# Units of 256 places in place of 512 in the edge list of a graph attention layer

## What is computed

```python
x = x + conv2d(bfp_quantize(layernorm_channels(x)), bfp_quantize(w), bias)   # 16 x 64 x 56 x 56
t = tokens(x)                                   # 50,176 rows of 64
h = ln(t) @ W_gat                               # 16 numbers per node: 4 heads x 4 experts
e = leaky_relu(a_src[src] + a_dst[dst])         # 262,144 edges, 4 heads each
alpha = exp(e - e_max[dst]) / denom[dst]
agg = segment_sum(h[src] * alpha, dst)          # per node
w = softmax of the top 2 of 4 experts of mean_heads(layernorm(agg))
out = t + sum over 4 experts of w[e] * (gelu(t @ W1[e] + b1[e]) @ W2[e] + b2[e])
```

## Time and profile before

| | |
|---|---|
| median of 3 runs | 4735.66 us (4731.93 to 4740.96) |
| the profiled execution's own time | 4737.77 us |
| its span | 4736.0 us |
| mean granted TensorE clock | 0.820 |
| PE busy | 82% of the span |
| POOL busy | 60% |
| DVE busy | 56% |
| ACT busy | 20% |

### The profile page before, as it was taken

How to read it: one execution, slowest core, us unless ns; L and a number is a source line. 1 busy time by engine, 2 the same in 40 slices (tenths; PEclk the granted TensorE clock), 3 DMA queues, 4 the chain that set the end, 5 groups by cost and what they waited for, 6 DMA issues and landing times. The chain is left out here.

```text
span 4736.0 us, 62817 instructions
## 1 busy us (share of the span) xinstructions
PE 3866.3 (82%) x21121; PEld 2690.0 (57%) x21121; DVE 2657.0 (56%) x3261; ACT 942.1 (20%) x2069; POOL 2844.5 (60%) x2881
## 2 busy tenths in 40 slices
PE   4785333799948999999999999999999999661499
PEld 1453223577736666666666666666666667561122
DVE  7779999667644444444444444444444444447666
ACT  0110000000012333332333333333333333110000
POOL 2001888766626777777777777777777777771000
PEclk8897555788867888988888988889888888776699
DMA  1232111788862111111111111111111111682498
GB/s 48 69 96 74 49 47 35 85 107 102 102 107 49 34 35 34 36 35 35 35 35 35 35 35 35 35 33 37 32 38 33 35 35 34 10 10 3 137 289 247
DMA packets 323403, 284.04 MB, mean 60 GB/s; under 512 B 201074, under 2 KB 279154, under 8 KB 322804
## 3 DMA queue, kind: packets, MB, share of 16 engines
q1 hardware_dynamic: 213732, 200.98, 19.9%
q0 software_dynamic: 91008, 30.58, 11.5%
q10 hardware_dynamic: 18576, 51.39, 2.8%
HBM read 160.41 MB, written 122.31 MB: 60 GB/s over the span
## 5 line engine op out<-in xcount | busy, mean ns | idle before, releaser
L1074 POOL DMA_INDIRECT gath<-tab_d,src_no x2288 | 2158.9, 944 | 775.8 <-issue 696.9
L446 POOL DMA_INDIRECT edge_d<-run_slots,slots x544 | 657.2, 1208 | 662.8 <-ACT run_slots L636 502.2
L1204 PEld LDWEIGHTS C<-spread,lo_hot 128*128 128x128 f32 x4576 | 848.1, 244 | 331.3 <-DVE spread L1359 173.7
L1204 PE MATMUL C<-spread,lo_hot 128*128 128x160 f32 x4576 | 920.2, 370 | 139.4 <-DVE spread L1359 139.1
L1193 PEld LDWEIGHTS C<-dst_rows,lo_hot_t 128*128 128x128 f32 x4576 | 586.7, 208 | 91.1 <-issue 78.3
L1371 DVE TENSOR_TENSOR acc<-acc,C 128x160 f32 x572 | 183.5, 321 | 796.3 <-PE C L1204 746.8
L1193 PE MATMUL C<-dst_rows,lo_hot_t 128*128 128x32 f32 x4576 | 603.9, 289 | 11.2 <-ACT lo_hot_t L1092 11.2
L1214 PE MATMUL A<-T,w1s 64*128 64x392 f32 x1024 | 533.8, 605 | 0.0
L1097 ACT ACTIVATE hid<-A,b1s 128x392 f32<-128x392 f32 x512 | 300.6, 587 | 1078.9 <-PE A L1214 1078.9
L557 PE MATMUL C<-wide_rec,hot_lo 128*128 128x136 f16 x2048 | 266.8, 305 | 296.9 <-DVE wide_rec L814 296.9
L1225 PE MATMUL A<-hid,w2s 128*64 128x392 f32 x1024 | 456.3, 528 | 0.0
(11 more groups left out here) (263 smaller groups left out, 3195.6 us busy)
## 6 DMA issues: line engine op xcount, KB each, us to landing
mlp_d<-mlp ACTq DMA_DIRECT2D x128, 392.0 KB
mlp<-mlp_d SPq DMA_DIRECT2D x64, 784.0 KB, 4.7
gath<-tab_d,src_no POOLq DMA_INDIRECT x2288
pixels<-in_x SPq DMA_DIRECT2D x32, 392.0 KB, 8.1
src<-in_x SPq DMA_DIRECT2D x32, 392.0 KB, 9.2
T<-t_d SPq DMA_DIRECT2D x128, 98.0 KB
X<-x_d SPq DMA_DIRECT2D x64, 196.0 KB, 5.4
out<-X SPq DMA_DIRECT2D x128, 98.0 KB, 2.6
```

The lines of the kernel that those rows point to most:

```text
L446: pool.indirect_dma_start(edge_d, bass.IndirectOffsetOnAxis(ap=slots[:, k, c:c + 1], axis=0), run_slots[:, k, c * RUN:(c + 1) * RUN, :].re ...
L1074: pool.indirect_dma_start(gath[:, g % BUFS, j, :], None, tab_d, bass.IndirectOffsetOnAxis(ap=src_no[:, t:t + 1], axis=0)).then_inc(gathere ...
L1204: mm = pe.matmul(C[:, bank, at:at + HI * VALS], lo_hot[:, k, u * U + j, :], spread[:, u * U + j].rearrange("p h v -> p (h v)"), start=(j = ...
```

## The change

A unit is 2 tiles of 128, that is 256 places, and takes 64 runs of 4. Lane l below 64 holds places 0 and 1 of run l, lane 64 + l holds places 2 and 3 of it. A group is 8 units, still 16 tiles. Filling blocks up to whole units takes fewer places, and NG is 137, TILES 2,192. The list in DRAM has 64 rows, and it is loaded twice, once into each half of the lanes, each time with all 4 places of a run (`raw`, which lies in the space of `lo_hot`); each field is then read from it in two copies, one for each half. PSUM holds four units at a time (two banks of two), so the 8 units of a group go in 4 pairs through the two banks by turns, and PE waits before each pair until DVE has added the pair before the last (`pair_added`). In PE's `body` the first half's transposes stand ahead of step 2, and the second half of the scatters behind it.

```diff
-U = 4
-UNIT_RUN_BITS = 7
-UG = 4
+U = 2
+UNIT_RUN_BITS = 6
+RUN_ROWS = U * P // RUN
+PARTS_U = P // RUN_ROWS
+UG = 8
+PAIRS = UG // 2
...
-PLACES = TILES // RUN
-ALL_PLACES = PLACES + SG * RUN_COLS
+PLACES = NG * UG
+ALL_PLACES = PLACES + SG * RUN_COLS * P // RUN_ROWS
...
-        edge_d = dram("edge_d", [P * ALL_PLACES, RUN * FIELDS], F16)
+        edge_d = dram("edge_d", [RUN_ROWS * ALL_PLACES, RUN * FIELDS], F16)
...
-                n = TILES * FIELDS // 8
+                n = PLACES * RUN * FIELDS // 8
                 for k in range(8):
-                    pool.dma_start(edge_d.rearrange("(p n) e -> p (n e)", p=P)[:, k * n:(k + 1) * n], zeros_h[:, 0:n].bitcast(F16)).then_inc(s["pads_written"], 16)
+                    pool.dma_start(edge_d.rearrange("(p n) e -> p (n e)", p=RUN_ROWS)[:, k * n:(k + 1) * n], zeros_h[0:RUN_ROWS, 0:n].bitcast(F16)).then_inc(s["pads_written"], 16)
...
-            srt = tb("srt", [P, TILES, FIELDS], F16)
...
-                return 1 + u // 2, u % 2 * HI * VALS
+                return 1 + u // 2 % 2, u % 2 * HI * VALS
...
-            TRIPS = -(-NG // UNROLL)
-            LAST = NG - (TRIPS - 1) * UNROLL
+            TRIPS = (NG - 3) // UNROLL
+            LAST = NG - TRIPS * UNROLL
...
-                sp.dma_start(srt[:].rearrange("p c k -> p (c k)"), edge_d.rearrange("(p n) e -> p (n e)", p=P)[:, 0:TILES * FIELDS]).then_inc(s["sorted_loaded"], 16)
+                for h in range(PARTS_U):
+                    sp.dma_start(raw[h * RUN_ROWS:(h + 1) * RUN_ROWS], edge_d.rearrange("(p n) e -> p (n e)", p=RUN_ROWS)[:, 0:PLACES * RUN * FIELDS]).then_inc(s["sorted_loaded"], 16)
...
-                def scatter(g, k, units):
-
-                    if units[0] == 0:
+                def scatter(g, k, pairs):
+
+                    if pairs[0] == 0:
                         pe.wait_ge(s["spread_ready"], g + 1)
-                    for u in units:
-                        bank, at = bank_of(u)
-                        for j in range(U):
...
-                        if u % 2:
-                            mm.then_inc(s["scattered"], 1)
+                    for w in pairs:
+                        if w >= 2 or not (isinstance(g, int) and g == 0):
+                            pe.wait_ge(s["pair_added"], g * PAIRS + w - 1)
+                        for u in range(2 * w, 2 * w + 2):
+                            bank, at = bank_of(u)
+                            for j in range(U):
...
+                        mm.then_inc(s["scattered"], 1)
...
                     mlp_step(0)
-                    scatter(g, k, range(0, 2))
+                    scatter(g, k, range(0, PAIRS // 2))
                     mlp_step(1)
-                    scatter(g, k, range(2, UG))
-                    mlp_step(2)
                     if turns:
                         turn(g + 2, k2, 0)
+                    mlp_step(2)
+                    scatter(g, k, range(PAIRS // 2, PAIRS))
                     mlp_step(3)
...
-                L(dve.tensor_copy(mixed_i, srt[:].bitcast(U16)[:, :, 0]))
+                def field(v, dt):
+
+                    for h in range(PARTS_U):
+                        a = slice(h * RUN_ROWS, (h + 1) * RUN_ROWS)
+                        yield (mixed_i[a].rearrange("p (n t) -> p n t", t=U),
+                               raw[a].bitcast(dt).rearrange("p (n t v) -> p n t v", t=RUN, v=FIELDS)[:, :, h * U:(h + 1) * U, v])
+                for to, code in field(0, U16):
+                    L(dve.tensor_copy(to, code))
...
-                L(dve.tensor_copy(mixed_i, srt[:, :, 1]))
+                for to, place in field(1, F16):
+                    L(dve.tensor_copy(to, place))
...
                         if u % 2 == 0:
-                            dve.wait_ge(s["scattered"], g * 2 + bank)
+                            dve.wait_ge(s["scattered"], g * PAIRS + u // 2 + 1)
                         here = acc[:, bass.ds(qs[u], HI), :]
                         L(dve.tensor_tensor(here, here, C[:, bank, at:at + HI * VALS].rearrange("p (h v) -> p h v", h=HI), ALU.add))
+                        if u % 2:
+                            dve.sem_inc(s["pair_added"], 1)
```

More of the change, by code:

```diff
@@ L83 @@
 ID_W = -(-NG * UG // P)
-PLACES = TILES // RUN
-ALL_PLACES = PLACES + SG * RUN_COLS
-assert 1 << RUN_BITS == RUN and 1 << UNIT_RUN_BITS == U * P // RUN == P
+PLACES = NG * UG
+ALL_PLACES = PLACES + SG * RUN_COLS * P // RUN_ROWS
+assert 1 << RUN_BITS == RUN and 1 << UNIT_RUN_BITS == RUN_ROWS and PARTS_U * U == RUN
 BLKS = NB + 1
@@ L737, in _ @@
                 L(dve.tensor_reduce(start_b[:], runs, AX.X, ALU.add))
-                L(dve.tensor_scalar(units_i[:], start_b[:], float(P - 1), None, ALU.add))
+                L(dve.tensor_scalar(units_i[:], start_b[:], float(RUN_ROWS - 1), None, ALU.add))
                 L(dve.tensor_scalar(units_i[:], units_i[:], UNIT_RUN_BITS, None, ALU.arith_shift_right))
@@ L753, in _ @@
                                     start_b[:].rearrange("p (b k) -> p b k", k=1).broadcast_to([P, NB, SG]), ALU.add))
-                L(dve.tensor_scalar(shift_g[:, :, NB], lane[:, 0:SG], float(P * RUN_COLS), float(P * PLACES), ALU.mult, ALU.add))
+                L(dve.tensor_scalar(shift_g[:, :, NB], lane[:, 0:SG], float(P * RUN_COLS), float(RUN_ROWS * PLACES), ALU.mult, ALU.add))
                 L(dve.tensor_copy(runs_g[:, :, 0:NB], runs.rearrange("p b g -> p g b")))
@@ L1152, in _ @@
                         body(i, k, True)
-                with act.Fori(MLP_TRIPS, TRIPS - 1) as i:
+                with act.Fori(MLP_TRIPS, TRIPS) as i:
                     for k in range(UNROLL):
@@ L1156, in _ @@
                 for k in range(LAST):
-                    body(TRIPS - 1, k, False, True)
+                    body(TRIPS, k, False, True)
                 for h in range(2):
@@ L1195, in pick_dst @@
                     mm.then_inc(s["picked_ready"], 1)
-                def scatter(g, k, units):
-                    if units[0] == 0:
+                def scatter(g, k, pairs):
+                    if pairs[0] == 0:
                         pe.wait_ge(s["spread_ready"], g + 1)
-                    for u in units:
-                        bank, at = bank_of(u)
-                        for j in range(U):
-                            mm = pe.matmul(C[:, bank, at:at + HI * VALS], lo_hot[:, k, u * U + j, :],
-                                           spread[:, u * U + j].rearrange("p h v -> p (h v)"), start=(j == 0), stop=(j == U - 1))
-                        if u % 2:
-                            mm.then_inc(s["scattered"], 1)
+                    for w in pairs:
[4 more added lines that the diff above has]
+                            for j in range(U):
+                                mm = pe.matmul(C[:, bank, at:at + HI * VALS], lo_hot[:, k % UNROLL, u * U + j, :],
+                                               spread[:, u * U + j].rearrange("p h v -> p (h v)"), start=(j == 0), stop=(j == U - 1))
+                        mm.then_inc(s["scattered"], 1)
                 def up(m, h, e):
@@ L1266, in _ @@
                         body(i, k, True)
-                with pe.Fori(MLP_TRIPS, TRIPS - 1) as i:
+                with pe.Fori(MLP_TRIPS, TRIPS) as i:
                     for k in range(UNROLL):
@@ L1387, in _ @@
                 spread_out(0, 0)
-                with rolled(dve, 0, TRIPS - 1, step, UNROLL * (4 + UG)) as i:
+                with rolled(dve, 0, TRIPS, step, UNROLL * (4 + UG)) as i:
                     for k in range(UNROLL):
@@ L1391, in _ @@
                 for k in range(LAST):
-                    body(TRIPS - 1, k, True)
+                    body(TRIPS, k, True)
                 agg, den = acc[:, :, 0:FEAT], acc[:, :, FEAT:VALS]
```

20 lines of the change are left out of this document (11 added, 9 removed).

## The result

| | before | after |
|---|---|---|
| median | 4738.31 us (4 runs, 4731.93 to 4742.18) | 4628.63 us (4 runs, 4621.27 to 4636.59) |
| the profiled execution's own time | 4737.77 us | 4624.48 us |
| its span | 4736.0 us | 4622.7 us |

The account below looks back on a forecast made before the run. POOL's gathers, at steps of 1.2483 us without waits, were taken as the bound, PE close behind. 4736.0 - 119.8 (gathers) + 3.5 (loads) + 0.4 (stage 1) = 4620.1 us of span; predicted 4620, range 4611 to 4645.

Parts of the forecast that it names:

- rival C: Start of stage 2: loads dearer, 10 us by half speed into 64 lanes, or DVE's casts uncovered; 4627 to 4632; chance 0.07.
- POOL sets the pace: Gather loop: POOL never waits, so 96 fewer gathers at 1.2483 us each take 119.8 us off.
- PE follows, with no new wait behind the experts: PE's bodies with experts: waiting for pairs costs nothing; the body stays 17.36 or 20.73 us.
- The margin of 0.7 us: PE with experts, upper clock: it reaches pair 2 0.7 us after DVE's add of pair 0 releases it.
- The way round through DVE: Last adds, `weigh`, next scatter: S + 14.2 us, or 17.6 with a clock fall, under 19.97; DVE's shrinking gather wait absorbs it.
- The loads, +3.5: Start of stage 2: 1.07 MB more of list ahead of the nodes, priced by a large store at 332 GB/s.
- One of the prediction's own signs against itself: Start of stage 2: nodes landing over 10 us later would mean the prediction is wrong, by C.
- Stage 1, +0.4: Two small DVE operations on the table of units grow from 245 to 441 numbers: +0.4 us, ends 0 and 1.
- The end, 0 to +2: Last gather to last add: pair 2 may wait for pair 0, mostly hidden by lower-clock scatters; 0, at most 2 us.
- Rival A: Groups with experts: clock falls in every body, PE takes over; about 4680, milder form about 4645; both together 0.12.
- B: PE's bodies: waits for pairs plus falling clock set the pace; slower, about 4870 with 22.3 us bodies; chance 0.04.
- D: List of units: the change doesn't shorten it; excluded by the fixed NG, chance under 0.01.

Follow-up runs that it names:

- b_ng137: Kernel before, units of 512, run over 137 groups in place of 143, nothing else changed: 6616.80 us, ratio 0.9775; repeated in another series, 6616.44 us, 0.978.
- b_half_loads: Kernel before, its list loaded in two DMAs of 64 lanes each, same bytes: 6686.45 us (before in that series 6692.35).
- b_twice: Kernel before with a second, unused load of 1.05 MB into 128 lanes behind the list's: 6718.17 us (before in that series 6692.35).

## Why the prediction was right

The forecast was 4620 us in a range of 4611 to 4645, faster with 0.95. It came to 4628.63: faster, 0.19% above the number and inside the range. Of the 8.6 us that it is off, 4.2 lie between the profiled execution and the median, 1.8 around its span, and 2.6 in the span (4620.1 forecast, 4622.7 measured). That the span came out so close is in part luck: the 2.6 are +8.0 and -5.5 that cancel, told below. And the median didn't come out within 1 us of the span but 5.9 over it, so that it lies where rival C had put it, 4627 to 4632, for another reason.

- **POOL sets the pace; a step is 1.2483 us; -119.8.** Right, -119.9. The size is shown by the profile after: the same step, and nothing but issue before 2,191 gathers. That it is the fewer groups and nothing else of the change is shown by b_ng137, in two series (-148 and -154, where a group lasts longer).
- **PE follows, with no new wait behind the experts.** Right as a result: no such wait, the body 20.67 for 20.73, clock 0.87 for 0.87. The margin of 0.7 us that stood behind it was worked out with register loads of 1.4 us; they took 1.0, so the margin is 1.1. Without experts the stall is 1.07 us in the group shown, predicted 1.6, and 0.4 of these 0.5 are the same register loads.
- **The way round through DVE.** Right: the wait for gathers shrank, by 1.9 us a group where about 3 was expected, and took it all up.
- **The loads, +3.5.** The mechanism was right (more bytes ahead of the nodes, everything hangs on the nodes), the size was off by a factor of two: +7.6. The step that failed is the choice of a store from all 128 lanes at 332 GB/s as the row for a load into 64. The bounds from above, 6 us for two loads at the old load's time and 10 with half the speed besides, were the nearer ones. Rival C had the right mechanism in its first half (the rate) and not in its second (DVE's casts kept their cover). One of the prediction's own signs against itself appeared: the nodes are used 11.9 us later than before (1413.74 for 1401.82), and over 10 was to mean C. Of these, 7.6 are the loads and 4.3 were there before the first of them. For the same reasons the first gather starts 11.8 us later, where 2 to 6 was to be the sign of being right, and the last one 108.1 us earlier, not 116.
- **Stage 1, +0.4.** Measured +4.3, and it can't be put down to the change: b_half_loads and b_twice, alike up to there and of one series, reach the list's load at 1536.89 and 1559.28 us. On those chips, at least, the scatter of stage 1 from one execution to the next is larger than the term.
- **The end, 0 to +2.** From `weigh` on +0.5, as said. What was not in the sum is that the last group's gathers landed 3.7 us sooner after their start. Why, no run tells. The -2.0 after the last add isn't explained either.
- **Rival A and B.** Neither came about in the condition for which they were forecast. On the experiments' chips POOL does wait for `rows_used`, the sign by which the prediction would have known them, and the changed kernel gained 0.85% in place of 2.3%. The kernel before waits there in the same way, so the change isn't the cause of the wait; but the 94 to 95 us that finer units cost there say that what the change adds to a group is not hidden everywhere; the profiles show it hidden behind the gathers only in their own condition.
- **D.** Excluded, and so it was.
- **Two ends of ranges** don't follow from the prediction's own terms: 4615.9 less 4 is 4612, not 4611, and C's 4632 is neither the 10 us (4627) nor the 8 us (4628) nor both (4635). Neither decides anything here.

## What to carry to other kernels

Price a stage by the engine whose instructions start at equal steps with nothing but issue before them: here such a step gave a term right to 0.1 us while the page's shares pointed at another engine. Such a price holds for the condition in which it was read: where the groups lasted longer the same six were worth 148 us, and what the change adds to a group was no longer hidden. To part two things that a change does, run all four combinations side by side. When a transfer changes the number of lanes that it fills, take its price from a row of the same lanes or from the bound, not from the nearest transfer of the same bytes; and look at which dimension comes first in a DMA before making one of two. Repeat the same kernel at another time before reading a difference of 1 to 2%, whatever the ratio's interval says.

## What the runs showed of the hardware that was not expected

- A load from DRAM into 64 lanes kept the DMA engines busy (0.92 and 1.00) at 213 GB/s; into 128 lanes 305 to 357 GB/s.
- One DMA whose source has a slowest dimension of 2 ran at 53 GB/s with the engines 0.12 busy, for 2.24 MB: the nodes 39 us later than before, where two DMAs cost 8.
- Eight register loads took 1.0 us and four 0.7: not twice.
- On two chips an add of DVE started 11.2 us after the recorded end of the matmul that it waited for, and regularly (42 groups) 3.2 to 4.3 us after POOL's last gather of the group; a group of 20 us took 33. The cause is open.
- On these chips the same kernel took 6571.08 us at a granted clock of 0.708 to 0.713 and 6720.06 at 0.691 to 0.694.
- With the nodes loaded first, some of POOL's first gathers took 1.5 to 2.2 us in place of 0.94.
